# Opening of a gated cross-attention kernel: the text projection is split, and two PSUM banks serve the turns

## The reference

```python
def layer0(features, txt, q_masks):                # features = layernorm(x)
    txt_proj  = txt @ Ws                           # (4, 64, 512)
    feat_proj = features @ W                       # (4, 1024, 512)
    h   = tanh(txt_proj[:, None] + feat_proj[:, :, None] + b)   # every token with every text token
    rho = h @ w + (1 - q_masks) * NEG
    att = softmax(rho, axis=-1)
    txt_h = att @ txt
    return tanh(txt_h @ Wcw.T + bcw) * features + tanh(txt_h @ Wcb.T + bcb)
x = x + tanh(g_xattn[0]) * layer0(layernorm(x), ctx_1024, mask)
...                                                # quantised feed-forward, attention, ternary feed-forward
```

## Time and profile before

| | |
|---|---|
| median of 3 runs | 1945.01 us (1943.3 to 1946.8) |
| profiled execution, its own time | 1944.79 us |
| span of its trace, first to last instruction | 1942.8 us |
| busy over the span | PE 1597.1, DVE 1711.3, ACT 1481.7, POOL 613.9 us |
| chain of work that ended last | ACT 43%, PE 35%, DVE 13% |
| largest line of that chain | ACT line 514, 40% |

### The profile page before, as it was taken

How to read it: one execution, slowest core, us unless ns; L and a number is a source line. 1 busy time by engine, 2 the same in 40 slices (tenths; PEclk the granted TensorE clock), 3 DMA queues, 4 the chain that set the end, 5 groups by cost and what they waited for, 6 DMA issues and landing times.

```text
span 1942.8 us, 24516 instructions
## 1 busy us (share of the span) xinstructions
PE 1597.1 (82%) x9510; PEld 719.8 (37%) x9510; DVE 1711.3 (88%) x2606; ACT 1481.7 (76%) x1105; POOL 613.9 (32%) x480
## 2 busy tenths in 40 slices
PE   6868965788556976786489987999999987899996
PEld 4212211122111321231144434666666653444442
DVE  6889998999999998889689886899999867999997
ACT  4899999999999999999644665454545336888781
POOL 1000000000000000000044225666666644899991
PEclk9999999999999999999889998999999999999999
DMA  5000200011000010000079765233333111122212
GB/s 203 1 1 23 87 12 0 23 52 41 6 1 1 17 49 12 1 3 10 0 248 354 262 221 155 92 115 109 99 115 100 56 55 40 45 77 76 66 55 76
DMA packets 116709, 143.65 MB, mean 74 GB/s; under 512 B 25326, under 2 KB 74606, under 8 KB 116210
## 3 DMA queue, kind: packets, MB, share of 16 engines
q1 hardware_dynamic: 116594, 142.10, 22.1%
HBM read 87.55 MB, written 50.33 MB: 71 GB/s over the span
## 4 chain that ended last, share of the span: by engine, by line
ACT 43%; PE 35%; DVE 13%; POOL 4%; issue 3%; DMA 2%; SPq 0%; DVEq 0%; POOLq 0%; ACTq 0%
ACT unit L514 40%; PE psum L1681 5%; PE psum L1715 5%; PE psum L1018 4%; PE psum L1012 4%; PE psum L1667 3%; DVE unit L423 2%; POOL h L1856 2%; PE psum L1738 2%; PE psum L1691 2%; PE psum L1708 2%; DVE psum L1447 1%; DVE psum L1452 1%; POOL hidden L1873 1%; PE psum L1700 1%
## 5 line engine op out<-in xcount | busy, mean ns | idle before, releaser
L514 ACT ACTIVATE unit<-unit 128x4096 f32<-128x4096 f32 x244 | 857.4, 3608 | 0.5 <-DVE unit L423 0.3
L423 DVE TENSOR_SCALAR unit<-feat_proj,text_proj 128x1024 f32<-128x1024 f32 x976 | 667.2, 746 | 67.1 <-PE psum L639 65.3
L639 PE MATMUL psum<-unit,w_pad 128*32 128x512 f32 x3904 | 474.6, 604 | 234.0 <-ACT unit L514 234.0
L639 PEld LDWEIGHTS psum<-unit,w_pad 128*32 128x32 f32 x3904 | 102.5, 109 | 556.9 <-ACT unit L514 398.7
L680 POOL TENSOR_SCALAR red<-red 128x8 f32<-128x8 f32 x4 | 2.0, 508 | 531.5 <-DVE red L321 531.5
L1738 PE MATMUL psum<-xq_block,w_q 128*128 128x512 bf16 x512 | 123.2, 386 | 14.2 <-ACT h L1614 11.0
L1856 POOL TENSOR_TENSOR h<-h,arow 128x512 f32<-128x512 f32 x104 | 125.8, 1233 | 20.1 <-ACT h L1614 20.1
L680 POOL TENSOR_SCALAR rstd<-mv 128x8 f32<-128x8 f32 (+1 forms) x5 | 1.7, 333 | 411.9 <-DVE mv L216 411.9
L547 PE MATMUL psum<-xnT,W_sb 128*128 128x512 f32 x256 | 125.2, 617 | 2.1 <-ACT xnT L465 2.1
L1589 ACT ACTIVATE scores<-scores 128x1024 f32<-128x1024 f32 x32 | 33.9, 1058 | 114.0 <-POOL scores L1842 114.0
L1873 POOL TENSOR_TENSOR hidden<-hidden,srow 128x2048 f32<-128x2048 f32 x28 | 114.3, 4084 | 9.8 <-DVE hidden_q L1482 9.7
(11 more groups left out here) (256 smaller groups left out, 2754.0 us busy)
## 6 DMA issues: line engine op xcount, KB each, us to landing
h_scratch<-h SPq DMA_DIRECT2D x44, 512.0 KB, 4.8
hin<-h_scratch SPq DMA_DIRECT2D x32, 704.0 KB, 4.6
xin<-in_x SPq DMA_DIRECT2D x8, 1024.0 KB, 6.7
tern_in<-in_w1T SPq DMA_DIRECT2D x16, 512.0 KB, 4.7
tern_in<-in_w2T SPq DMA_DIRECT2D x16, 512.0 KB, 6.2
x<-in_x SPq DMA_DIRECT2D x16, 512.0 KB, 3.7
x_scratch<-x SPq DMA_DIRECT2D x32, 256.0 KB, 2.0
x3in<-x_scratch SPq DMA_DIRECT2D x31, 256.0 KB, 3.0
```

The costliest lines, as they stand in the source:

```text
L423: ins = ve.tensor_scalar(units[:, n % 3, k, :], FP[:, bi % 2, k, :], TP[:, k, n:n + 1], None, ALU.add)
L514: ac.activation(units[:, n % 3], units[:, n % 3], ACT.Tanh).then_inc(unit_tanh, 1)
L639: mm = te.matmul(psum[k * TG:(k + 1) * TG, 3 + 2 * grp + half, :], w_pad[:, k, TG - 1 - tt:2 * TG - 1 - tt], units[:, n % 3, k, half * BAN ...
```

## The change

The text projection is split: text tokens 0 to 63 (batch 0) are projected first of all on PE, ahead of the turns, in matmuls of 64 columns; the other 192 tokens follow inside the unit loop at n = 13, 14, 16, 17, and the text rows, in four pieces, at n = 18, 20, 21, 22. Their copies move from ACT to DVE, at n = 19, 22 and 27. The turns of batch 0 alternate between banks 0 and 7. On DVE the first normalises are no longer separated by `largest`; the normalises of tiles 4 to 7 stand in the loop over k, and the turns of tiles 4 and 5 come after projection 1, of 6 after 2, of 7 after 3. ACT begins with a sigmoid of a constant tile, whose result is overwritten later, and computes the gates after the loop over k. POOL clears `v_diag` before the roots. SP loads `w` and `b` right behind the first x.

```diff
+    TURN0_BANK = (0, 7)
+    NORMALISED_AFTER = ((4, 5), (6,), (7,), ())
+    TURNED_AFTER = ((), (4, 5), (6,), (7,))
+    TEXT_REST = (13, 14, 16, 17)
+    TEXT_ROWS = (18, 20, 21, 22)
+    TEXT_LAG = 5
+    TEXT_DONE = 2 * KC + 2
+    def rest_bank(m):
+        return psum[:, 5 + m // 2, m % 2 * (NU - TXT):(m % 2 + 1) * (NU - TXT)]
...
 # vector_A
+        def text_rest(n):
+            for m in (1, 3):
+                if n == TEXT_REST[m] + TEXT_LAG:
+                    V.wait_ge(text_mm, KC + m + 1)
+                    for c in (m - 1, m):
+                        ins = ve.tensor_scalar(TP[:, c, TXT:NU], rest_bank(c), small[:, 1, c:c + 1], None, ALU.add)
+                    ins.then_inc(text_copied, 2)
+            if n == TEXT_ROWS[-1] + TEXT_LAG:
+                V.wait_ge(text_mm, 2 * KC + 2)
+                for r, row in enumerate((cw_row, cb_row)):
+                    ins = ve.tensor_copy(row[:, :], psum[:, 7, r * NU:(r + 1) * NU])
+                ins.then_inc(text_copied, 2)
...
-        for q in range(2):
-            for i in range(q * TPK, (q + 1) * TPK):
-                moments(0, i)
-            aggregate(0, q * TPK, (q + 1) * TPK)
-            for i in range(q * TPK, (q + 1) * TPK - q):
-                normalise(0, i)
-                if i <= TPK:
-                    largest(0, i)
+        for i in range(TPK):
+            moments(0, i)
+        aggregate(0, 0, TPK)
+        for i in range(TPK):
+            if i == TPK - 1:
+                largest(0, 0)
+            normalise(0, i)
+        for i in range(1, TPK):
+            largest(0, i)
+        for i in range(TPK, TPB):
+            moments(0, i)
+        aggregate(0, TPK, TPB)
...
             for u in range(SLOTS):
                 ramp_add(u, k, k + 1)
-            if k == 0:
-                normalise(0, TPB - 1)
-            else:
-                largest(0, TPK + k)
+            for i in NORMALISED_AFTER[k]:
+                normalise(0, i)
+            largest(0, TPK + k)
             moments(1, k)
...
 # scalar_A
-        for i in range(TPK):
-            turned(i)
+        A.wait_ge(ident_done, 1)
+        ac.activation(sig[:, :], half_neg[:, 0:2], ACT.Sigmoid)
         A.wait_ge(early_loaded, NEARLY)
         for m in range(KC):
             A.wait_ge(text_mm, m + 1)
-            ac.activation(TP[:, m, :], psum[:, 3 + m, 0:NU], ACT.Identity, bias=small[:, 1, m:m + 1]).then_inc(text_copied, 1)
+            ac.activation(TP[:, m, 0:TXT], psum[:, 3 + m, 0:TXT], ACT.Identity,
+                          bias=small[:, 1, m:m + 1]).then_inc(text_copied, 1)
+        for i in range(TPK):
+            turned(i)
+        for k in range(KC):
+            projected(k)
+            for i in TURNED_AFTER[k]:
+                turned(i)
+            for u in range(SLOTS):
+                ramp_tanh_of(u, k, k + 1)
         A.wait_ge(const_loaded, NCONST)
         ac.activation(sig[:, :], clips[:, :], ACT.Sigmoid).then_inc(gates_done, 1)
         ac.activation(tg[:, :], gates[:, :], ACT.Tanh).then_inc(gates_done, 1)
-        for k in range(KC):
-            projected(k)
-            turned(TPK + k)
-            for u in range(SLOTS):
-                ramp_tanh_of(u, k, k + 1)
...
-            if u == 2 * RAMP - 4:
-                for r, row in enumerate((cw_row, cb_row)):
-                    A.wait_ge(text_mm, KC + r + 1)
-                    ac.activation(row[:, :], psum[:, 7, r * NU:(r + 1) * NU], ACT.Copy).then_inc(text_copied, 1)
...
 # tensor_A
+        def text_first(m):
+            T.wait_ge(text_loaded, 32)
+            for k in range(KC):
+                mm = te.matmul(psum[:, 3 + m, 0:TXT], Ws_sb[:, k, m * P:(m + 1) * P], ctx_sb[:, k, 0:TXT],
+                               start=(k == 0), stop=(k == KC - 1))
+            mm.then_inc(text_mm, 1)
...
+            T.wait_ge(xnT_copied, t if bi else t - 1)
+            bank = 0 if bi else TURN0_BANK[i % 2]
...
+        for m in range(KC):
+            text_first(m)
         for i in range(TPK):
             turn(0, i)
-        T.wait_ge(text_loaded, 32)
-        for m in range(KC):
-            for k in range(KC):
-                mm = te.matmul(psum[:, 3 + m, 0:NU], Ws_sb[:, k, m * P:(m + 1) * P], ctx_sb[:, k, :],
-                               start=(k == 0), stop=(k == KC - 1))
-            mm.then_inc(text_mm, 1)
         for k in range(KC):
             project(0, k, 0, KC)
-            turn(0, TPK + k)
+            for i in TURNED_AFTER[k]:
+                turn(0, i)
         for j in range(KC):
             project(0, KC + j, 0, KC)
             ramp_rho(2 * j)
             ramp_rho(2 * j + 1)
-        text_rows()
...
 # gpsimd_A
         G.wait_ge(ident_done, 1)
+        gp.memset(v_diag[:, :, :, :], 0.0).then_inc(v_zeroed, 1)
...
 # sync_A
         load_x(0, 0)
+        for dst, src in ((small[:, 0, :], w), (small[:, 1, :], b)):
+            sp.dma_start(dst, src).then_inc(early_loaded, 16)
         sp.dma_start(ctx_sb[:, :, :], ctxT).then_inc(text_loaded, 16)
         sp.dma_start(Ws_sb, Ws).then_inc(text_loaded, 16)
         sp.dma_start(W_sb[:, :, :], W).then_inc(W_loaded, 16)
-        for dst, src in ((small[:, 0, :], w), (small[:, 1, :], b)):
-            sp.dma_start(dst, src).then_inc(early_loaded, 16)
```

More of the change, by code:

```diff
@@ L294, in tail @@
                 if s == at:
-                    V.wait_ge(text_copied, KC + 2)
+                    V.wait_ge(text_copied, TEXT_DONE)
                     V.wait_ge(tail_step, done + ATT_INV + 2 * n)
@@ L334, in tail @@
                 ve.tensor_tensor(ln1_max[:, ts], ln1_scale[:, ts], xn_max[:, ts], ALU.mult).then_inc(tail_step, 1)
+        def text_rest(n):
+            for m in (1, 3):
+                if n == TEXT_REST[m] + TEXT_LAG:
+                    V.wait_ge(text_mm, KC + m + 1)
+                    V.wait_ge(early_loaded, NEARLY)
+                    for c in (m - 1, m):
[6 more added lines that the diff above has]
+                ins.then_inc(text_copied, 2)
         def weights(slot):
@@ L419, in vector_A @@
             V.wait_ge(unit_mm, n - 2 - RAMP)
+            if n == TXT:
+                V.wait_ge(text_copied, 2 * KC)
             if n < RAMP + 3:
@@ L430, in vector_A @@
                 prep(bi + 1, t)
+            text_rest(n)
             weights(n)
@@ L464, in turned @@
             A.wait_ge(xnT_filled, i + 1)
-            ac.activation(xnT[:, :, i * P:(i + 1) * P], psum[:, 0, :].rearrange("p (k t) -> p k t", k=KC),
+            ac.activation(xnT[:, :, i * P:(i + 1) * P],
+                          psum[:, TURN0_BANK[i % 2], :].rearrange("p (k t) -> p k t", k=KC),
                           ACT.Copy).then_inc(xnT_copied, 1)
@@ L518, in tensor_A, with text_rest @@
     def tensor_A():
-        def text_rows():
-            T.wait_ge(const_loaded, NCONST)
-            for r in range(2):
-                for k in range(KC):
-                    mm = te.matmul(psum[:, 7, r * NU:(r + 1) * NU], small[:, 2 + r, k:k + 1].broadcast_to([P, P]),
-                                   ctx_sb[:, k, :], start=(k == 0), stop=(k == KC - 1))
-                mm.then_inc(text_mm, 1)
+        def text_first(m):
[4 more added lines that the diff above has]
+            mm.then_inc(text_mm, 1)
+        def text_rest(n):
+            for m, at in enumerate(TEXT_REST):
+                if n == at:
+                    T.wait_ge(text_copied, KC)
+                    for k in range(KC):
+                        mm = te.matmul(rest_bank(m), Ws_sb[:, k, m * P:(m + 1) * P], ctx_sb[:, k, TXT:NU],
+                                       start=(k == 0), stop=(k == KC - 1))
+                    mm.then_inc(text_mm, 1)
+            for j, at in enumerate(TEXT_ROWS):
+                r, part = divmod(j, 2)
+                if n == at:
+                    T.wait_ge(const_loaded, NCONST)
+                    T.wait_ge(xnT_copied, TPB)
+                    for k in (2 * part, 2 * part + 1):
+                        mm = te.matmul(psum[:, 7, r * NU:(r + 1) * NU], small[:, 2 + r, k:k + 1].broadcast_to([P, P]),
+                                       ctx_sb[:, k, :], start=(k == 0), stop=(k == KC - 1))
+                    if part == 1:
+                        mm.then_inc(text_mm, 1)
         def turn(bi, i):
@@ L530, in turn @@
             T.wait_ge(xn_done, t + 1)
-            T.wait_ge(xnT_copied, t)
+            T.wait_ge(xnT_copied, t if bi else t - 1)
+            bank = 0 if bi else TURN0_BANK[i % 2]
             for k in range(KC):
-                tr = te.transpose(psum[:, 0, k * P:(k + 1) * P], xn[:, t % 3, k * P:(k + 1) * P], ident[:, :])
+                tr = te.transpose(psum[:, bank, k * P:(k + 1) * P], xn[:, t % 3, k * P:(k + 1) * P], ident[:, :])
             tr.then_inc(xnT_filled, 1)
@@ L564, in rho_sum @@
             T.wait_ge(start_step, 2)
-            T.wait_ge(text_copied, KC + 2)
+            T.wait_ge(text_copied, TEXT_DONE)
             T.wait_ge(tail_step, (bi - 1) * TAIL_STEPS + RHO_MASKED)
@@ L686, in gpsimd_A @@
```

(1 more changed line is left out.)

## The result

The changed kernel took 1938.53 us, the median of 5 executions (1935.68 to 1939.6), against 1945.01 before: ratio 0.9961, 95% interval 0.9949 to 0.9974. The forecast was 1934.5 with a range of 1932.0 to 1941.0: the sign is right, the range holds it, but the gain is 6.5 us where 10.3 were forecast, and the time lies nearer to rival B (1939.8). A second comparison gave 0.9943 (0.993 to 0.9956): medians of 1936.57 against 1946.81, about 10 us. One of its six executions of the changed kernel took 2055.65 us at a lower clock, and one of the kernel before 9086.42; the ratio leaves both out.

The account below looks back on a forecast made before the run. ACT's tanh chain was taken to bound stage A, so bringing ACT earlier moves its end one for one. From 1944.8 us, -7.0 + 0.3 - 1.8 - 1.2 - 0.6 = -10.3 gave 1934.5; own range 1932.5 to 1936.5, with rivals 1932.0 to 1941.0.

Parts of the forecast that it names:

- rival B: Opening on PE: clock stays low through text and turns, projection 0 at 23.0 and slow (+1.8); 1939.8 us in all; chance 0.22.
- Item 1: Text projected first on PE: starts at 10.6, steps of 0.225 us at the low clock, then 0.115 at the high.
- Item 2: Four turns through two banks, ACT's copies following each other: projection 0 starts at 19.5 instead of 26.53, -7.0 us.
- item 3: Loop over k, end of projection 0 to projection 4: same work, but turns 4 and 5 come together, +0.3 us.
- item 4: Projection 4 on PE: without the 2.1 us idle before it, full clock, 3.63 us for 5.40, -1.8.
- item 5: Text rows out of the ramp: ACT's 1.24 us idle before 74.33 closes, -1.2, and its copies leave, -0.6.
- item 6: Unit loop takes the moved work on DVE and PE within a lead of 2.3 us: 0.
- DVE's cover: Loop over k: DVE had 6.73 us to spare; the change spends it, with no wait, within 0.5 us.
- Rival D: Unit loop, n = 13 to 22: PE at low clock under the moved work, 1948.0 us; slower by over 0.2% has 0.03.
- C: Opening: narrow products at the wide form's pace, 1937.5 us, chance 0.08; or x of batch 1 late, 1936.5, 0.06.
- E: Ramp held by something unseen, or stages B and C give the gain back: only -2 to -3, 1942 us; chance 0.05.

Follow-up runs that it names:

- the warmed kernel: The changed kernel with 28 constant products (ident x ident) on PE ahead of the text projection: 1935.6 us, ratio 0.9939; in the second comparison 1932.43 us, 0.9927.

## Why the prediction was right or wrong

Right in sign and range; the term that failed is the clock inside items 1 and 2. At the first unit the first profile of the changed kernel shows -5.9 where the sum had -10.3:

| step | forecast | measured |
|---|---|---|
| projection 0 starts (items 1, 2) | 19.5, -7.0 | 22.09, -4.4 |
| projection 0 itself | 0 | 5.30 for 3.45, +1.85 |
| loop over k (item 3) | +0.3 | 27.39 to 41.79, 14.4 for 14.2: +0.2 |
| projection 4 (item 4) | -1.8 | -1.7 |
| text rows (item 5) | -1.2 - 0.6 | -1.86 |
| unit loop (item 6) | 0 | 0 (idle 0.3 in both) |

The span fell by 0.6 more behind the first unit, within what that part scatters (1849.3 to 1852.8 over the profiles). That the second comparison gave about 10 us, all but the forecast 10.3, is luck: its profiled opening was only 7.4 ahead of the first profile of before, and the rest is scatter behind the first unit and between executions.

**Item 1.** The start (10.6, measured 10.66) and the slow step (0.225, measured 0.22) were right, and so was the quick step (0.115, measured 3.68 / 32). The failed step is "I take as long a low stretch as these rows show, 3.8 us". In none of the profiles with this opening did the text speed up; the low stretch was 7.1 us of text, then most or all of the turns, and in one profile of four the first half of projection 0. I had transferred the length of a low stretch from 256- and 512-column work to 64-column work, and had written down myself, in rival B, that this was shown nowhere. The reading was narrow, too: with the turns and their gaps counted, the rows of before show a low stretch from 11.61 to 21.2, 9.6 us. B deserved more than its 0.22, though its last term, +1.8 for projection 0, came in one profile of four: without it the first unit is at 85.4, 7.4 to 7.6 ahead of before.
**Item 2.** Turns at the low clock came 0.9 apart, not the 1.1 that B used: 17.74 to 21.33 for four, so projection 0 started at 22.09 and not at B's 23.0. With B's other terms that gives 1938.9, the measured time within 0.4. At full clock item 2 was sized rightly: the warmed kernel needs 3.1 us from the end of the text to projection 0, where the forecast had 3.3.

**Items 3 and 5** held. DVE's cover held better than I gave it: its wait before the first add was 4.24 us of the former 6.73, and 1.80 in the warmed kernel. **Item 4** held in the profile, but its cause, a lowered clock before the change, is only at times there; after the change projection 4 took 3.70 in every profile. **Item 6** held, with room for the four text slots' work once more at a price of 2 us, in one execution. Rival D was priced for a clock that stayed low; it rose within unit 12, which took 3.38 us, as the 3.29 of before. Rivals C and E are out: with warm PE the narrow form has its own pace, DVE never waited for x of batch 1, and the gain of the opening arrives unchanged at the last unit of stage A.

## What to carry to other kernels

Where a kernel's first matmuls are on the critical path, ask which clock they will run at, and don't borrow the length of the low stretch from work of another shape; constant products in PE's idle time ahead of them (here 28 of them, until the weights land) took 4.3 to 6.4 us off the opening, depending on which profiles are compared, about half of what reordering alone had promised. When work is moved off the path into a saturated loop, compute the lead that the buffers give, then double the work once to see whether it is real. A gain in an opening should be read at a mark right behind it, since what comes later scatters by 3.5 us here (1849.3 to 1852.8), half of what the opening gained.

## What was not expected of the hardware

In the opening the granted clock does not tell the speed. Windows over the text products, changed kernel and then warmed kernel:

```profile
10.60:17.70 7.10, 7.04 (x33) 7.05 (x34) 2.05 (x4) 0.94 (x3) 0.38 (x1) 1.00 0.79 268
```
```profile
10.90:14.60 3.70, 3.70 (x36) 3.70 (x35) 1.99 (x4) 0.94 (x3) 0.00 (x0) 1.00 1.00 390
```

Both say 1.00, with the same instructions at 0.22 and 0.115 us each. Only the pace, about half, shows that the first runs at the lower level, 1.2 GHz, and the second at 2.4. Later drops, as in projection 4 of before, do stand in that column.

Idle for 2.12 us ahead of projection 4, PE kept its clock once and lost it twice. Idle for 2.4 ahead of unit 12, it lost it in nine profiles and kept it in two. In the other two of the thirteen it had lost it before, though since projection 4 no idle time there had been longer than 1.27 us. PE in the kernel with the text rows back, the last half units of the ramp, and a window in them:

```profile
83.31 1.07 PE L641 MATMUL psum<-unit,w_pad 128*32 128x512 f32 x8 [1.27 <-ACT unit L491]
85.11 3.69 PE L641 MATMUL psum<-unit,w_pad 128*32 128x512 f32 x16 [0.74 <-ACT unit L491]
```
```profile
86.00:87.00 1.00, 1.00 (x12) 0.09 (x8) 1.00 (x3) 1.00 (x2) 0.00 (x0) 0.50 0.00 0
```

So the length of the one idle time just before does not tell whether the clock falls, and item 4's argument from 1.59 us of idle time was weaker than it looked. What tells these executions apart stays open; so does what makes stage B scatter beyond the one window shown.
